# Three planned times change the order on GpSimd: convolution later, pair products earlier, partners on a semaphore of their own

## The reference, cut to what matters

```
x = inp.reshape(B, G, CPG, H, Wd)
p2 = x[:, :, _I2] * x[:, :, _J2]
p3 = x[:, :, _I3] * x[:, :, _J3] * x[:, :, _K3]
return inp + y2 * beta2 + y3 * beta3 * CONV3_SCALE
...
g = jnp.clip(_bn(conv1x1(l, w_inside), gamma1, beta1, mean1, var1), 0.0, 6.0)
theta = l[:, :c_red]
f = jnp.einsum('niab,nicd->nabcd', theta, theta)
f = jax.nn.softmax(f.reshape(n, h * w, h, w), axis=1)
f = jax.nn.softmax(f.reshape(n, h * w, h * w), axis=2)
out = jnp.einsum('nabcd,nicd->niab', f, g)
out = depthwise3x3(out / h * w, w_dw)
return _bn(out, gamma2, beta2, mean2, var2) + l
```

## Time and profile before

| what | value |
|---|---|
| median of 3 runs | 5255.1 us (5251.17 to 5261.56) |
| the profiled execution | 5256.16 us, its span 5254.2 us |
| busy in the span: PE, PEld | 5045.8 us (96%), 2352.9 us (45%) |
| busy in the span: ACT, POOL, DVE | 4672.5 us (89%), 4566.2 us (87%), 4445.8 us (85%) |
| mean granted TensorE clock | 0.987 |
| DMA engines | 0.4 to 0.5 of the time in most slices |

### The profile page before, as it was taken

One profiled execution on the slowest core, in us unless ns is written; L12 is line 12 of the kernel. 1 busy time (PEld: TensorE's weight loads), 2 busy tenths in 40 slices (PEclk: granted clock), 3 DMA queues, 4 the chain that ended last, 5 costly groups with the idle time before them and its releaser, 6 DMA issues.

```text
span 5254.2 us, 91825 instructions
## 1 busy us (share of the span) xinstructions
PE 5045.8 (96%) x32492; PEld 2352.9 (45%) x32492; DVE 4445.8 (85%) x8615; ACT 4672.5 (89%) x2508; POOL 4566.2 (87%) x1654
## 2 busy tenths in 40 slices
PE   9899999999999999999999999999999999999999
PEld 3444444444444444444444444444444444444444
DVE  8788888888888888888888888888888888888887
ACT  8688989988998898899899998898988898898998
POOL 6459898988898899889989888899898989878997
PEclk9899999999999999999999999999999999999999
DMA  8544555444555454555454455444555454454211
GB/s 167 128 111 102 143 139 135 122 121 123 129 140 132 111 123 111 140 127 143 119 125 124 122 134 135 119 124 112 134 128 140 116 131 116 122 132 94 62 30 41
DMA packets 419511, 631.28 MB, mean 120 GB/s; under 512 B 183350, under 2 KB 371823, under 8 KB 413552
## 3 DMA queue, kind: packets, MB, share of 16 engines
q1 hardware_dynamic: 417952, 624.53, 48.4%
q10 hardware_dynamic: 1104, 0.89, 0.1%
HBM read 519.21 MB, written 102.74 MB: 118 GB/s over the span
## 4 chain that ended last, share of the span: by engine, by line
PE 48%; POOL 18%; issue 15%; ACT 8%; DVE 4%; SPq 4%; DMA 3%; DVEq 0%; POOLq 0%
PE at_AV L1669 21%; PE at_S L1602 13%; POOL at_ZP L1287 7%; PE at_AV L1675 7%; POOL at_OUTB L1317 5%; ACT at_ring L1352 5%; ACT at_ring L1358 4%; POOL at_ZB L1308 2%; DVE at_ring L1442 2%; PE at_S L1626 2%; PE l_TY L824 2%; POOL at_XI L1291 2%; DMA at_ZB<-rzd 2%; PE at_AV L1633 2%; PE at_AV L1665 1%
## 5 line engine op out<-in xcount | busy, mean ns | idle before, releaser
L1442 DVE TENSOR_SCALAR_CACHE_REDUCE at_ring<-at_S 128x1344 f32<-128x1344 f32 (+2 forms) x2352 | 2893.0, 1241 | 263.7 <-PE at_S L1602 240.0
L1352 ACT ACTIVATE at_ring<-at_ring,at_NM 128x3136 f32<-128x3136 f32 x784 | 2278.6, 2906 | 526.1 <-DVE at_NM L1454 522.6
L1669 PE MATMUL at_AV<-at_ring,at_GT 128*64 128x392 f32 x12800 | 2352.4, 504 | 22.5 <-DVE at_ACC L1550 4.9
L1287 POOL TENSOR_TENSOR at_ZP<-at_ZP,at_ring 128x1568 f32<-128x1568 f32 x640 | 2264.0, 3570 | 51.8 <-ACT at_ring L1358 43.5
L1358 ACT ACTIVATE at_ring<-at_ring,at_RZ 128x3136 f32<-128x3136 f32 x784 | 2273.0, 2899 | 0.7 <-DVE at_RZ L1462 0.7
L1602 PE MATMUL at_S<-at_THM,at_THS 128*128 128x448 f32 x5376 | 1434.1, 392 | 48.7 <-DVE at_ring L1442 24.1
L1669 PEld LDWEIGHTS at_AV<-at_ring,at_GT 128*64 128x64 f32 x12800 | 834.5, 137 | 1252.7 <-issue 1054.3
L1602 PEld LDWEIGHTS at_S<-at_THM,at_THS 128*128 128x128 f32 x5376 | 920.7, 189 | 765.9 <-DVE at_ring L1442 339.1
L1317 POOL TENSOR_TENSOR at_OUTB<-at_OUTB,at_ZB 128x1568 f32<-128x1568 f32 x246 | 879.9, 3577 | 16.8
L1675 PE MATMUL at_AV<-at_ring,at_ones 128*32 128x392 f32 x6656 | 645.0, 501 | 12.1 <-DVE at_ACC L1550 4.5
L1552 DVE TENSOR_TENSOR at_ACC<-at_AV,at_ACC 128x392 f32<-128x392 f32 x772 | 432.6, 561 | 115.3 <-PE at_AV L1669 108.2
(11 more groups left out here) (106 smaller groups left out, 2599.9 us busy)
## 6 DMA issues: line engine op xcount, KB each, us to landing
at_XB<-in_x SPq DMA_DIRECT2D x672, 224.0 KB, 3.7
at_XI<-in_x SPq DMA_DIRECT2D x336, 224.0 KB, 2.9
at_XJ<-in_x SPq DMA_DIRECT2D x504, 112.0 KB, 2.8
at_THM<-hld SPq DMA_DIRECT2D x128, 392.0 KB, 7.3
at_THS<-hld SPq DMA_DIRECT2D x256, 192.0 KB, 3.8
at_CIN<-att SPq DMA_DIRECT2D x62, 406.0 KB, 7.0
at_ZB<-rzd SPq DMA_DIRECT2D x62, 406.0 KB, 7.9
att<-at_ACC SPq DMA_DIRECT2D x248, 98.0 KB
```

Source lines behind the costliest of these rows:

```text
L1287: e.tensor_tensor(z, z, v, ALU.add).then_inc(g_add, 1)
L1352: e.activation(v, v, ACT.Exp, bias=NM[:, i:i + 1], accum_out=ZS[:, i:i + 1]).then_inc(a_p1, 1)
L1442: e.tensor_scalar(ring[:, s % RING, SC * a_:SC * b].rearrange("p (b w) -> p b w", w=SC), PS[:, p.run_slot[k] % 2, bank:bank + b - a_, 0:SC ...
L1669: ins = e.matmul(dst[64 * j:64 * j + 64, 0:QC], GT[fl.n % 2][:, keys_of(fl.n, t), :], ring[:, slot, q:q + QC], start=(i == 0), stop=(i == ...
```

## The change

Three assumed times of the plan change, and one load is split. `PAIR_LAT` goes from 14000 to 8000. The t step is planned 3000 ns behind its product, where it was 60 (`PROD_LAT`). The convolution is planned 40000 ns behind the image's sums, where it was 20000 (`CONV_LAT`). `pair_in` keeps the two loads of `at_XI`; the three of `at_XJ` become `partner_in`, which waits for product k - 1 on POOL in place of products k - 1 on PE, has its own semaphore and its own place in SP's order, and the product waits for both semaphores. No instruction is added or removed on PE, DVE, ACT or POOL, apart from waits; all of them except ACT get another order.

```diff
-PAIR_LAT = 14000
+PAIR_LAT = 8000
+CONV_LAT = 40000
+PROD_LAT = 3000
...
     def pair_ready(k):
-        return pair_issue(k) + PAIR_LAT
+        return max(pair_issue(k), partner_issue(k)) + PAIR_LAT
+
+    def partner_issue(k):
+        return end_p.get(k - 1, inf) if k else 0.0
...
-                v = max(tp, free, free_slot(q - 2), end_p.get(n_t, inf) + LAT, factor_ready(n_t) + LAT,
+                v = max(tp, free, free_slot(q - 2), end_p.get(n_t, inf) + PROD_LAT, factor_ready(n_t) + LAT,
...
-            cg.append((max(tg, image_end.get(conv[0][0], inf) + 20000), 1, "conv"))
+            cg.append((max(tg, image_end.get(conv[0][0], inf) + CONV_LAT), 1, "conv"))
...
             def pair_in(k):
                 n, w = of_step(k)
                 if k:
                     e.wait_ge(pe_f, fill_of("t", k - 1) + 1)
+                for t in range(2):
+                    e.dma_start(XI[:, t, :], x[n, 32 * t:32 * t + 32, w].unsqueeze(1).broadcast_to([32, 4, SC])).then_inc(s_pair, 16)
+
+            def partner_in(k):
+                n, w = of_step(k)
+                if k:
+                    e.wait_ge(g_p2, k)
                 else:
                     e.wait_ge(g_one, 1)
-                for t in range(2):
-                    e.dma_start(XI[:, t, :], x[n, 32 * t:32 * t + 32, w].unsqueeze(1).broadcast_to([32, 4, SC])).then_inc(s_pair, 16)
                 for d, src in ((1, x), (2, xs[2]), (3, xs[3])):
-                    e.dma_start(XJ[d:128:4, :, :], src[n, :, w].rearrange("(t c) w -> c t w", t=2)).then_inc(s_pair, 16)
+                    e.dma_start(XJ[d:128:4, :, :], src[n, :, w].rearrange("(t c) w -> c t w", t=2)).then_inc(s_part, 16)
...
             def product(k):
-                e.wait_ge(s_pair, 80 * (k + 1))
+                e.wait_ge(s_pair, 32 * (k + 1))
+                e.wait_ge(s_part, 48 * (k + 1))
```

More of the change, by code:

```diff
@@ L516, in plan @@
         at["pair", k] = pair_issue(k)
+        at["partner", k] = partner_issue(k)
         at["factor", k] = factor_issue(k)
@@ L957, in build @@
         s_pair = sem("pair")
+        s_part = sem("part")
         s_fac = sem("fac")
@@ L1190, in _ @@
                     for k in range(CT * (n - first_moved), CT * (n - first_moved + 1)):
+                        todo.append((at["partner", k], partner_in, (k,)))
                         todo.append((at["pair", k], pair_in, (k,)))
```

## The result

| | before | after |
|---|---|---|
| median of 5 runs each, side by side | 5260.2 us (5251.17 to 5266.08) | 5237.52 us (5232.7 to 5240.56) |
| the profiled execution, span | 5256.16, 5254.2 us | 5237.97, 5235.7 us |
| PE busy, span less busy | 5045.8, 208.4 us | 5037.4, 198.3 us |
| mean granted clock | 0.987 | 0.987 |

The ratio is 0.9953, interval 0.994 to 0.9966: 0.5% faster, where 1.4% was forecast. The time lies above the forecast's own range (5138 to 5215), in the stretch that the prediction gave to rival one (5215 to 5244), and so inside the wide range of 5140 to 5244, near its upper end.

What follows compares the result with a forecast made beforehand. PE was taken to bound the kernel, with only its idle time and lost clock to win: 5256.2 - 57 - 26 - 6 + 15 = 5182 us profiled, median 5181. Own range 5138 to 5215 (chance 0.60); 8 in 10: 5140 to 5244.

Steps and rivals of the forecast that it cites:

- rival one: Half of the 83 us won returns as PE's waits for DVE, ACT or loads: 5207 to 5222 us, chance 0.20.
- What bounds the kernel: PE sets the time with fixed work; only its idle time, 208 us, and lost clock can be won.
- Products forward, -57: Products earlier on POOL and 3 us ahead of t cut PE's product waits from 76.7 to 20 us: -57 us.
- The convolution at 0: Moving the convolution back on POOL nearly ends its stall for at_ZB, at no direct PE cost: 0, bounds -5 and +15.
- The clock, -26: On PE, clock dips behind long product waits mostly vanish: -26 of 33.1 us, bounds 0 and -33.
- Shapes, -6: PE's list has 43 rows less, so fewer changes of tile shape: -6 us, bounds 0 and -8.
- Partners' rows at 0: SP's added wait for product k - 1 cannot hold the loads and stores behind it for long: cost 0.
- What is late next, +15: PE, arriving earlier, waits more for DVE and the values' loads: +15 us, a quarter of three small causes' 61 us.
- Rival two: PE does not set the pace, ACT does, so PE's waits are slack: 5250 us, chance 0.08.
- Rival three: Channels' rows land late, POOL stands at the product and PE waits: slower, 5257 to 5300 us and more, chance 0.12.
- tell-tales: Signs named beforehand for the profile after: product waits, at_ZB wait, clock and PE's busy share, plus one for each rival.

Runs made afterwards that it cites:

- b_const: The kernel before, with PE's t step reading a constant so it never waits for POOL's product: 5186.64 us, ratio 0.9856.
- a_pair14: The changed kernel with PAIR_LAT at 14000 again: 5205.02 us, ratio 0.9903.
- a_prod60: The changed kernel with PROD_LAT at 60 again, the t step planned directly behind its product: 5230.80 us, ratio 0.9941.
- b_conv40: The kernel before with only the convolution's planned place moved from 20000 to 40000 ns: 5232.02 us, ratio 0.9950.
- a_conv20: The changed kernel with CONV_LAT at 20000 again: 5277.28 us, ratio 1.0026.
- a_accsp: The changed kernel with the stores of an image's sums sorted 5 us earlier in SP's order: 5190.78 us, ratio 0.9864.
- a_acclate: The changed kernel with the stores of an image's sums sorted 3 us later in SP's order: 5298.28 us, ratio 1.0072.
- a_joined: The changed kernel with the partners' rows issued right behind pair_in again in SP's order: 5224.11 us, ratio 0.9930.
- a_plan: The changed kernel with sums' stores 5 us earlier and DVE's first copy of an image's sums planned behind the previous image's last sum: 5187.16 us, ratio 0.9855.
- pair14_plan: a_plan with PAIR_LAT at 14000: 5175.54 us, ratio 0.9840.
- a_best: a_plan with PROD_LAT at 60: 5192.42 us, ratio 0.9872.

## Why the prediction was partly wrong

**What bounds the kernel: right.** PE's waits set the time; taking the product waits away alone gave 76.7 us, 1.4% (b_const).

**Products forward, -57: the waits went further, by another hand.** They fell by 75.3, not 57. But the count of POOL's work ahead of each product ascribed it to `PAIR_LAT` and the 3 us, and each can be undone with next to none coming back (a_pair14 5.0 us, a_prod60 3.6); b_conv40, with neither, has 13.6. At step 68 the forecast holds as written: PE in order of time in after shows

```profile
2070.47 0.60 PE L1640 MATMUL at_S<-at_XI,at_WT 32*64 32x448 f32 x3 [0.59 <-POOL at_XI L1305]
```

where 3.96 us stood. So the count was right that the products would be in time, and wrong about which part of the change would do it.

**The convolution at 0: wrong.** The step said that the stall for `at_ZB` (172.5 us) should nearly vanish, which it did, and that it "costs PE nothing directly". It was the main source: with the late convolution alone 63 of the 76.7 us of product waits go (b_conv40), and without it 44.2 come back (a_conv20). While POOL stood at `at_ZB`, additions and products behind it stood too. The mechanism was named and not priced. Its bounds of -5 and +15 don't hold what b_conv40 and a_conv20 show, 26 us and 38 us.

**The clock, -26: mis-sized and moved.** The clock column fell by 7.5 only, from 56.3 to 48.8. The dips behind product waits went, and dips behind the image ends came: 3.4 us of the column lay at ends before, 10.8 do now. The term also took length times (1 - clock) at face value; b_const shows 17.2 of busy time for 23.5, and a_accsp and a_acclate, which have one order on PE, 42.6 for 56.7: three quarters in both. It is a mean and no constant: after, with that same order, lies at 16.4 for 17.4 from the one and 26.2 for 39.3 from the other. And a fall of 7.5 in one execution is inside what executions of one kernel differ by; all executions on record together, with mean clocks of 0.986 before and 0.987 after, lie about as far apart.

**Shapes, -6: not measured apart.** At three quarters, 7.5 us of clock make an estimated 5.6 of the 8.4 that PE's busy time fell. 2.8 are left for 43 changes of shape (1.3 to 3.4 by the two other shares), inside the bounds of 0 and -8. No run shows this term by itself.

**Partners' rows at 0: wrong, 12 us (a_joined).** "It cannot hold them for long" was argued for the store of a y, the factors, keys and values. The stores of the sums stand behind it too and were not in the list, and they are what an engine waits for. For the products the early rows bought nothing that shows: joined, 3.4 us of product waits are left, and 1.4 apart.

**What is late next, +15: the step that failed.** The sum by the trace is -75.3 of product waits, +65.2 of other waits, and by the estimate above -5.6 of clock and -2.8 of shapes: -18.5, the difference of the spans. The forecast's was -57, +15, -26, -6. So this term was 50 us too small, and with it fell the clock's. It took a quarter of three small causes of the earlier trace rows and asked only which waits were already large for PE. It did not ask what DVE waits for: 49.0 us for its own old stores, in 22 of the 31 image changes, of which PE's rows for L1550 showed 9.4.

Two runs divide the 65.2. In b_const PE comes earlier by all 76.7 us and every order stays as before, and only 22.8 us of other waits come in: that is what the term asked for, and 15 was near. The other 42 came with the new orders. The steps on the convolution and on the partners' rows looked for such a price on POOL and on SP, put both at 0 and left out the sums' stores. Moving these stores alone takes 31.5 us of other waits away again (a_accsp: 170.2 idle with 4.7 of product waits, after: 198.4 with 1.4), 47 us of time with the clock. The late convolution, the early products and the partners' place each make the stores later; their prices (idle at ends 48.1 with the first alone, 26 us, 12 us) overlap and can't be added.

**The rivals.** Rival one, given back, is what happened, in size (5222, or 5237 measured) and in sort: PE's waits for DVE. By its tell-tale (above 100 us) the rows above come to 116; the same six came to 64 before. But it took the half that is given back for what full engines do; a_accsp shows that most of it hung on the order of one queue. Rival two fell with b_const. Rival three's first sign came, POOL waiting 132.4 us for `at_XI` where 60 was the mark; its second, product waits above 60, did not, so its price at PE is nearly nothing: its argument that t steps stand far apart held. Of the tell-tales, the product waits came out below the 10 to 30 named, the `at_ZB` wait was right, and the clock (0.992 or more; 0.987 in this execution) and busy share (97%; 96) failed; a_plan and pair14_plan, without the late stores, have 0.991 and 97%. The text's last sentence, that it is wrong if product waits vanish and the time does not follow, describes the result.

## What to carry to other kernels

Before pricing the removal of a wait, look at the other engines' waits that end at the same events, also those which cost nothing yet: here DVE's 49 us for a buffer's own stores became 68 when PE alone came earlier, and 92 in the new order. Then ask what the new order does to a queue that issues in order: for each entry, who waits for its landing, and does anything now stand ahead of a store that frees a single buffer. Test the remedy in the order in which it is to stand: the same move of the stores took 47 us off the kernel after and put 15 on the kernel before. And a part of a change that is counted only as safety for another part deserves a price of its own: moved alone, the convolution gave the whole gain.

## What the runs showed of the hardware

**A wait's length does not settle whether the clock dips.** In the kernel before, PE waits 2.24 us for a product at 1779 us and again at 1900. The five microseconds from each (columns as in the earlier trace rows):

```profile
1779.00:1784.00 5.00, 4.74 (x51) 1.56 (x51) 3.63 (x4) 2.67 (x1) 4.92 (x3) 1.00 0.97 211
1900.00:1905.00 5.00, 4.66 (x27) 1.80 (x29) 2.88 (x4) 2.86 (x2) 4.92 (x3) 0.66 0.37 113
```

The first keeps 2.4 GHz throughout, the second falls to 1.2 GHz for a part. In after PE around 3067 us has three waits, none of them over 2.05 us, and a dip too:

```profile
3066.78 0.87 PE L1689 MATMUL at_AV<-at_ring,at_ones 128*32 128x392 f32 x8 [2.05 <-DVE at_ACC L1564]
3068.31 1.13 PE L1616 MATMUL at_S<-at_THM,at_THS 128*128 128x448 f32 x3 [0.67 <-DVE at_ring L1456]
3070.12 1.49 PE L1616 MATMUL at_S<-at_THM,at_THS 128*128 128x448 f32 x3 [0.69 <-DVE at_ring L1456]
```

```profile
3064.00:3074.00 10.00, 6.60 (x32) 2.26 (x30) 7.23 (x16) 5.55 (x4) 10.00 (x3) 0.74 0.14 40
```

The clock over the 10 us is 0.74, so part of it ran at 1.2 GHz, and by the third row three matmuls take 1.49 us where they took 0.87. Whether the two short waits behind the first helped to bring it about, no run tests.

**Among executions of one kernel, time and clock move together.** The 45 executions of the kernel before have means of 5250.8 us at a granted clock of 0.988, 5259.8 at 0.986 and 5267.9 at 0.984: 17 us for 21 us of clock, some four fifths. And kernels with much the same idle time can differ in clock: a_best has 170.5 us idle in the span and 0.990 to 0.992 in its four runs, a_pair14 174.1 and 0.987 to 0.989 in its five.
